# Attention and mixture-of-experts block: where the first batch's leftover projections, the second batch's statistics and the last batch's residual steps stand in the order

## Time and profile before

| what | value |
|---|---|
| median of 3 runs | 976.48 us (976.4 to 976.97) |
| the profiled execution, its device time | 975.89 us |
| its span, first to last instruction | 974.1 us |
| mean granted clock of TensorE | 0.968 |
| TensorE, VectorE, ScalarE, GpSimd busy | 876.2, 790.7, 668.4, 324.3 us |

### The profile page before, as it was taken

One profiled execution on the slowest core, in us unless ns is written; L12 is line 12 of the kernel. 1 busy time (PEld: TensorE's weight loads), 2 busy tenths in 40 slices (PEclk: granted clock), 3 DMA queues, 4 the chain that ended last, 5 costly groups with the idle time before them and its releaser, 6 DMA issues. The chain is left out here.

```text
span 974.1 us, 14309 instructions
## 1 busy us (share of the span) xinstructions
PE 876.2 (90%) x5164; PEld 317.1 (33%) x5164; DVE 790.7 (81%) x1564; ACT 668.4 (69%) x735; POOL 324.3 (33%) x462
## 2 busy tenths in 40 slices
PE   6879999999999999999999999999988989875995
PEld 3312222222243233222332243322421413144784
DVE  4588879898979878889889879889799788446785
ACT  5128878787877777888778878878687768931210
POOL 4043010005425323129434423237253141653033
PEclk9779999999999999999999999999999989997998
DMA  5631010310230303101522022004410000242001
GB/s 144 107 42 40 16 56 15 71 42 10 81 74 12 94 13 67 42 13 26 105 71 62 7 45 55 25 10 94 99 49 24 13 8 16 68 168 65 1 0 66
DMA packets 52439, 49.11 MB, mean 50 GB/s; under 512 B 17536, under 2 KB 43760, under 8 KB 51984
## 3 DMA queue, kind: packets, MB, share of 16 engines
q1 hardware_dynamic: 51744, 46.95, 19.5%
q0 software_dynamic: 384, 1.05, 0.3%
q10 hardware_dynamic: 240, 0.20, 0.2%
HBM read 18.10 MB, written 9.17 MB: 28 GB/s over the span
## 5 line engine op out<-in xcount | busy, mean ns | idle before, releaser
L1348 DVE TENSOR_REDUCE mx<-ring 128x1 f32<-128x512 f32 x1024 | 634.0, 682 | 110.4 <-PE ring L1062 109.8
L896 ACT ACTIVATE prob<-sc,unscale 128x1024 f32<-128x1024 f32 x512 | 539.6, 1114 | 84.7 <-PE sc L1080 83.5
L1062 PE MATMUL ring<-kp,qp 48*128 48x512 f16 x1024 | 299.4, 395 | 43.3 <-DVE mx L1348 22.4
L1094 PE MATMUL obank<-prob,vaug 128*32 128x512 f32 x2048 | 276.1, 612 | 0.7 <-ACT prob L896 0.6
L1062 PEld LDWEIGHTS ring<-kp,qp 48*128 48x128 f16 x1024 | 74.2, 93 | 360.9 <-DVE mx L1348 300.8
L1080 PE MATMUL sc<-qp,kp 64*128 64x512 f16 x1024 | 168.0, 381 | 14.0 <-ACT prob L896 13.3
L654 POOL TENSOR_TENSOR parts<-qkf,parts 128x1024 f16<-128x1024 f32 x14 | 29.9, 2133 | 205.0 <-ACT parts L826 205.0
L1080 PEld LDWEIGHTS sc<-qp,kp 64*128 64x128 f16 x1024 | 50.4, 95 | 92.8 <-ACT prob L896 84.6
L641 POOL TENSOR_TENSOR hid<-hid,b 128x512 f32<-128x512 f32 x24 | 30.3, 1272 | 110.5 <-ACT hid L850 110.5
L649 POOL TENSOR_TENSOR yA<-yA,sums 128x512 f32<-128x512 f32 x15 | 19.0, 1269 | 131.8 <-DMA sums<-reciprocal_scratch 131.8
L1094 PEld LDWEIGHTS obank<-prob,vaug 128*32 128x32 f32 x2048 | 40.4, 108 | 61.5 <-issue 58.0
(11 more groups left out here) (228 smaller groups left out, 749.9 us busy)
## 6 DMA issues: line engine op xcount, KB each, us to landing
x_sb<-x SPq DMA_DIRECT2D x7, 1024.0 KB, 5.9
kp<-parts SPq DMA_DIRECT2D x48, 128.0 KB, 4.4
qp<-parts SPq DMA_DIRECT2D x93, 64.0 KB, 5.4
out<-hid SPq DMA_DIRECT2D x4, 1024.0 KB, 5.3
yA<-oT SPq DMA_DIRECT2D x124, 32.0 KB
sums<-reciprocal_scratch SPq DMA_DIRECT2D x31, 128.0 KB
x_scratch<-x SPq DMA_DIRECT2D x3, 1024.0 KB, 4.5
qp<-mp SPq DMA_DIRECT2D x128, 2.0 KB
```

Of the source, the lines that this page charges most:

```text
L896: nc.scalar.activation(prob[:, e % 2, 2 * a:2 * a + 2, :].rearrange("p g n -> p (g n)"), sbuf2[a][:, :], ACT.Exp, scale=unscale[:, 0:1]).t ...
L1062: nc.tensor.matmul(dst[:, :], qp[rows, qh, h, qt * P:(qt + 1) * P], kp[rows, h, kh * HALF:(kh + 1) * HALF], start=True, stop=True).then_in ...
L1094: ins = nc.tensor.matmul(obank[i * VW:(i + 1) * VW, :], vaug[:, b % 2, kt, c0:c0 + VW], prob[:, v % 2, i, :], start=(kt == 0), stop=(kt == ...
L1348: nc.vector.tensor_reduce(mx[:, u % 2, n:n + 1], src[:, :], AX.X, ALU.max).then_inc(rv_free, 1)
```

## The change

1. **Lead items.** The first is made before slot 0, straight behind the value projections. The other three are made as single products (one of the two k halves each) in slots 0 to 5, between the two pairs of max products. ScalarE takes the items in slots 0, 1, 3 and 5.
2. **Statistics of batch 1.** `load_x(1)` moves on SyncE from behind the stacking DMAs to the place between the constant loads and the first stacking DMA. VectorE makes all 8 `bn_stats` before slot 0, and GpSimd runs `z_chain(1)` ahead of the two second parts.
3. **Last residual steps.** Normalize y and the add of half 0 follow the statistics of i = 2, those of half 1 the statistics of i = 3.
4. **Gathers.** On GpSimd the power for x of half 1 moves behind the four gathers. On VectorE h0 and "normalize x" of half 1 stand between the statistics of gathered tiles 1 and 2, and h1 behind `mean_of("m")`.
5. **End.** The last add and the store go by halves of the rows, the second half behind `stats("o", 0)`. On GpSimd both powers for o come ahead of the wait for the store, and all four scatters behind it.

More of the change, by code:

```diff
@@ L975, in project @@
                 ins.then_inc(r_full, 1)
-            def keys_or_queries(dst, c, h):
+            def keys_or_queries(dst, c, h, ks=range(KD)):
                 w, mt = (wk, wq)[c % 2], c // 2
-                for k in range(KD):
+                for k in ks:
                     ins = nc.tensor.matmul(dst[:, :], w[:, k, mt * P:(mt + 1) * P], zT[:, k, h * HALF:(h + 1) * HALF],
@@ L1421, in _ @@
                         ring_item(key)
-                if w + 1 < B:
-                    for i in slots_of(tau, Z_STATS[w > 0]):
+                if 1 <= w and w + 1 < B:
+                    for i in slots_of(tau, Z_STATS):
                         if i == 0:
```

## The result

The changed kernel takes 967.44 us, the median of 5 runs (964.27 to 967.64), against 976.48 for the kernel before (5 runs, 976.25 to 977.21). The ratio is 0.9896 with a 95% interval of 0.9882 to 0.9911: faster by 9.0 us. The forecast was 966.2 (964.4 to 970.4). The profiled execution took 967.64 us, its span 965.8, which is 8.3 less than before.

What follows compares the result with a forecast made beforehand. VectorE's row maxima bound slots 0 to 11, all four engines run near full from slot 12, and single engines wait on one another late. Gains 8.0 + 1.2 + 1.1 = 10.3 us; forecast 966.2 us, range 964.4 to 970.4.

Steps and rivals of the forecast that it cites:

- the start: Up to slot 12: lead items 5.27 us plus statistics 2.76 us, so slot 12 comes 8.0 us earlier.
- Lead items and the clock: Slots 0 to 7: VectorE's gaps of 5.27 us for TensorE vanish, with full clock and at most one cold slot (0.85).
- the row from 46 to 58 us: Profile row with granted clock 1.00 while lead items lay between max products; taken as nearest to changed slots 0 to 5.
- rival 1: Clock swings in slots 0 to 5, each cold slot costing 0.85 us: 968.8, up to 971.3 us; chance 0.20.
- The warm half item: Six half items of about 0.86 us at full clock, covered by VectorE's maxima: cost 0, at most 0.4 us.
- Statistics of batch 1: Two 1.38 us statistics leave slots 9 and 10 for idle time before slot 0: 2.76 us gained, load costing 0 (bound 0.5).
- Rival 4: Moved load is served together with the stacking copies and delays them 7.9 us: 982 us, slower; chance 0.03.
- Slot 12: First scores come 8.0 us earlier; the maxima's rows keep 2.7 us of slack, so a wait of 0 to 0.2, taken as 0.
- rival 3: Slot 12 waits for the rows of the maxima, 2 us in place of the time won: 968.2 us; chance 0.06.
- Residual steps and gathers: Last batch: residual steps gain 0.3 us, gathers start 2.0 us earlier; gain 1.2 us together, the 0.3 included.
- The end: Last 20 us: halved last add and store, four scatters in one run; last scatter 1.1 us earlier (bounds 0 and 1.5).
- The rest of the run: From slot 12 on everything moves along with the 8.0 us, since no step there waits for anything but slots.

Runs made afterwards that it cites:

- the second batch of runs: Runs made on chip number 4; the changed kernel, unchanged, ran again there: 969.23 us (967.7 to 969.98, 5 runs), ratio 0.9928.
- the third: Third batch of runs, on chip number 11; the changed kernel, unchanged, ran again there: 966.36 us (965.01 to 968.15, 4 runs), ratio 0.9902.
- the products in slots 0 to 5: Changed kernel plus two overwritten 48-row TensorE products a slot in slots 0 to 5: 964.76 us, repeated at 965.53 us.
- the second half add moved: Changed kernel with the last add of the second half behind the first routed result instead of ahead: 965.87 us, ratio 0.9907.
- last batch's part alone: Kernel before with only the changes after the last slot (residual steps, gathers, end): 973.12 us, ratio 0.9971.

## Why the prediction was right, and where not

- **Direction and size**: right. 967.44 lies in the range, 1.2 us above the forecast. It lies so near in part by luck: the start missed its sum by 3.1 us, and 1.1 us came from the middle, for which nothing was forecast. In the second batch of runs the same kernel gained 6.4 us (969.23 against 975.59), in the third 9.8.
- **Lead items and the clock**: this step failed. The mechanism, and 7.3 of the 8.0 us, hold in the executions where the clock lasts through slot 5: 30.08 us from the first maximum to the first scores in four profiles (the changed kernel in the third batch, the products in slots 0 to 5 twice, the second half add moved). With the lead items alone, where 2.6 us of statistics still stand in the slots, it took 32.68. The step that named the row from 46 to 58 us as the nearest, "full clock through these slots", doesn't hold in every execution: the clock fell at 41.8 us, and rival 1 came true in part. The busy share by which the row was chosen was much the same in both places, and so couldn't tell them apart. Rival 1's price was too low as well: a cold slot cost 1.45 us (1.17 where the clock fell within it) and not 0.85. The 2.51 of slot 4 from which 0.85 was worked out was not a wholly cold item's: that item's four products took 3.36 us, as the clock rose at 44.9, and a wholly cold one takes 3.78 and leaves a gap of 3.15 (last batch's part alone). Half a cold item is 3.78 less 2.07, so 1.7, and 3.15 less 1.7 is the 1.45 that was measured. Two cold slots made 2.9 us. Executions differ in this, and the runs of the changed kernel spread over 964.3 to 970 us.
- **The warm half item**: taken as 0, at most 0.4 for all six, with 0.06 worked out from slot 5. One maximum in each of these slots starts 0.14 later, which makes 0.8 us over six slots.
- **Statistics of batch 1**: 2.6 of 2.76 us left the slots at once, and the load cost nothing: the first max product starts no later. Rival 4 fell: the stacking copies kept their 132 to 140 GB/s. Alone the step was worth 1.8 us; in its profile the gap of slot 4 was 0.5 longer.
- **Slot 12**: the first scores came straight when VectorE's part allowed, so rival 3 fell.
- **Residual steps and gathers**: forecast 0.3 and 0.9, measured 0.5 and 1.1 (6.0 to 6.5 and 6.5 to 7.7 in the table of marks). The pieces (0.65 of delay, 1.5 of waiting) measured 0.5 and 1.42.
- **The end**: forecast 1.1, measured 0.6. The store was in time, as argued. The failed step: that `routed_result(0)` ends at 962.0: GpSimd's step on the means of pair 0 was held up 0.9 us by the very add that had been moved beside it, and `combine(1)` started 0.7 us behind TensorE's last product and not with it. That the last 110 us gave 2.3 in sum, as forecast, is two errors that cancel: 0.5 more ahead of the hidden layer and in the gathers, 0.5 less in the end.
- **The rest of the run** was taken to move along rigidly. It gave 1.1 us more in this execution: 0.4 were lost in slots 12 to 16, where the granted clock came up 7.5 us behind the first scores and not 5.8 as before, and about 1.4 won from 725 to 820 us, 1.0 of them at the fall of the clock that now hits other work. Together: 10.3 forecast, less 2.9 for the cold slots, 0.6 for the warm halves of slots 0 to 3, 0.2 for the statistics and 0.5 for the end, plus 0.4 at the first maximum, 0.5 in the residual steps and gathers and 1.1 in the middle, is 8.1, of the 8.3 measured.

Still open: what decides the moment at which the clock falls, which was 40.9 us in one execution and 50.6 in another of the same program, and whether the added products of slots 0 to 5 have a part in it.

## What to carry to other kernels

Work for TensorE that lies between small products belongs where the engine's clock is up, ahead of the stretch in which it falls; count such an item at both clocks, with the slow price for everything in its slot. When an addition is moved into the time that a small GpSimd step needs, the two are not independent; compare the placements by how long the last stage takes, from one fixed mark to another.

## What the runs showed that was not expected

- A TensorE busy for 4.00 of 4 us with products of 48 rows had its clock fall to 0.50, and one as busy with 128-row products among them kept 1.00 through the same slots (one profile and two).
- One program's executions differ by up to 7 us (969.27 to 976.17, lead items alone), and the slower ones have the lower mean clock, while the kernel before, whose items are made late, stays within 1.6 us over 20 runs.
- A GpSimd step on 128x2 elements took 1.07 in place of 0.19 us beside a VectorE addition of two SBUF operands.
